# Opening a transformer block kernel: the channel attention of two batches interleaved, raw rows and centred weights

## The reference, cut to what matters

```python
x = x + attn_a(layernorm(x))     # channel attention, 8 heads of 16 channels
x = x + ffn(layernorm(x))        # 8 experts, 336 hidden units each, all computed
x = x + attn_b(layernorm(x))     # attention over the 512 rows
x = x + ffn(layernorm(x))

# attn_a: rms norm, then
qkv = einsum('bnc,oc->bno', xn, w_qkv)
q, k = l2norm(q), l2norm(k)      # over the 512 rows
sim = einsum('bhin,bhjn->bhij', q * exp(temperature), k)
out = einsum('bhij,bhjn->bhin', softmax(sim), v)
return einsum('bnc,oc->bno', out, w_out)
```

## Time and profile before

| | |
|---|---|
| median of 3 runs | 487.98 us (487.86 to 488.89) |
| the profiled execution | 489.73 us |
| its span in the trace | 487.9 us |
| PE busy | 476.1 us |
| PEld, DVE, ACT, POOL busy | 342.7, 303.0, 266.2, 312.4 us |
| first feed-forward product (`gu 0`) | 23.39 us after the span's start |

### The profile page before, as it was taken

How to read it: one execution, slowest core, us unless ns; L and a number is a source line. 1 busy time by engine, 2 the same in 40 slices (tenths; PEclk the granted TensorE clock), 3 DMA queues, 4 the chain that set the end, 5 groups by cost and what they waited for, 6 DMA issues and landing times.

```text
span 487.9 us, 6499 instructions
## 1 busy us (share of the span) xinstructions
PE 476.1 (98%) x2039; PEld 342.7 (70%) x2039; DVE 303.0 (62%) x718; ACT 266.2 (55%) x484; POOL 312.4 (64%) x326
## 2 busy tenths in 40 slices
PE   8899899999999999999999999999999999999997
PEld 7777666677676666666676766677676777778886
DVE  3656342646487768499836884359754565666563
ACT  3395636646724693348742649235772456456551
POOL 5355789336948576486463466467675586778774
PEclk9999899999999999999999999999999999999999
DMA  7700000000000000000000000000000000000000
GB/s 240 247 0 2 0 1 0 1 1 1 1 0 2 1 0 1 1 1 1 0 1 0 1 2 0 1 1 5 19 0 2 0 23 1 0 1 10 15 0 22
DMA packets 7933, 7.36 MB, mean 15 GB/s; under 512 B 732, under 2 KB 7772, under 8 KB 7900
## 3 DMA queue, kind: packets, MB, share of 16 engines
q1 hardware_dynamic: 7900, 6.96, 4.4%
HBM read 5.91 MB, written 1.05 MB: 14 GB/s over the span
## 4 chain that ended last, share of the span: by engine, by line
PE 83%; ACT 2%; DVE 1%; POOL 1%; issue 0%; ACTq 0%; DVEq 0%; POOLq 0%
PE bank L1313 21%; PE bank L1128 17%; PE bank L1130 17%; PE bank L1129 17%; PE bank L1351 3%; PE bank L1249 1%; PE bank L1343 1%; PE bank L1151 1%; PE bank L1363 1%; PE bank L1321 1%; PE bank L1257 1%; PE bank L1291 1%; ACT L778 1%; PE bank L1239 0%; PE bank L1219 0%
## 5 line engine op out<-in xcount | busy, mean ns | idle before, releaser
L647 POOL TENSOR_TENSOR t<-t,sl 128x512 f32<-128x512 f32 x105 | 148.6, 1421 | 80.9 <-DVE t L1069 61.7
L778 ACT ACTIVATE sl<-bank 128x512 f32<-128x512 f32 x168 | 99.2, 596 | 126.3 <-PE bank L1130 114.5
L1313 PE MATMUL bank<-t,WD 128*128 128x512 f32 x256 | 126.0, 592 | 0.0
L1069 DVE TENSOR_TENSOR t<-bank,sbc 128x512 f32<-128x512 f32 x105 | 72.3, 689 | 72.2 <-PE bank L1130 70.5
L1128 PE MATMUL bank<-xhF,WGh 128*128 128x512 f32 x167 | 89.8, 538 | 1.0 <-ACT sl L778 0.9
L647 POOL TENSOR_TENSOR t<-t,sbc 128x512 f32<-128x512 f32 x63 | 79.4, 1288 | 0.2
L1069 DVE TENSOR_TENSOR t<-bank,sl 128x512 f32<-128x512 f32 x63 | 42.9, 686 | 55.8 <-ACT sl L778 30.0
L1128 PE MATMUL bank<-xhF,WUh 128*128 128x512 f32 x168 | 66.8, 397 | 1.1 <-DVE t L1069 1.1
L1130 PE MATMUL bank<-xhF,WUl 128*128 128x512 f32 x168 | 66.3, 395 | 0.0
L1129 PE MATMUL bank<-xlF,WUh 128*128 128x512 f32 x168 | 66.3, 394 | 0.0
L1130 PE MATMUL bank<-xhF,WGl 128*128 128x512 f32 x167 | 66.2, 397 | 0.0
(11 more groups left out here) (210 smaller groups left out, 722.9 us busy)
## 6 DMA issues: line engine op xcount, KB each, us to landing
stage<-in_gate SPq DMA_DIRECT2D x7, 192.0 KB, 5.7
stage<-in_up SPq DMA_DIRECT2D x7, 192.0 KB, 5.7
WD<-in_down SPq DMA_DIRECT2D x7, 192.0 KB, 5.7
X<-in_x SPq DMA_DIRECT2D x4, 256.0 KB, 5.4
out<-X SPq DMA_DIRECT2D x3, 256.0 KB, 2.3
raw<-in_small SPq DMA_DIRECT2D x1, 384.0 KB, 4.2
out<-X SPq DMA_DIRECT2D x2, 128.0 KB, 1.9
raw<-in_small SPq DMA_DIRECT2D x1, 192.0 KB, 2.7
```

The source lines that it names most:

```text
L647: pool.tensor_tensor(t2[k % NT2][:, :], t2[k % NT2][:, :], by[:, :], ALU.mult).then_inc(a_done, 1)
L778: act.activation(sl[k % NSL][:, :], bank[k % 2][:, :], ACT.Silu).then_inc(silu_done, 1)
L1069: dve.tensor_tensor(t2[k % NT2][:, :], bank[2 + k % 2][:, :], by[:, :], ALU.mult).then_inc(t2_done, 1)
L1313: r = pe.matmul(OACC[:, :], WD[:, c, :], t2[k % NT2][:, :], start=(c == 0), stop=(c == CH - 1 or k == TAIL[0] - 1))
```

## The change

Batch 0 and batch 1 both run through the whole channel attention in the hand-written opening, interleaved. `A1_STEPS` is gone.

- The rows are not normalised for the attention. The weights for q, k and v are multiplied on PE by a centred matrix (`cenw`: 1/128 minus the identity, times the norm weight): step `wn`, one product of 128 x 384 and a ScalarE copy. The Gram matrix is of raw rows with rows scaled by 1/(variance term) (`rinv`, two small VectorE operations in place of GpSimd's power); the transposes are of raw `X`; the factor `rstd` is applied when the result is added to x.
- Batch 0 has no `am2`: its values are projected first (step `vT`, one 128 x 512 product, into the tile `YT`), and `y` uses `mix` directly.
- The sums of squares are a step of their own (`asq`), in other banks.
- The head mask is written in three operations on 128 columns.
- Warming is 4, 3, 2 and 8 products at four places.
- A step `silu` applies Silu to one column, into a tile that nobody reads, ahead of the first real one.
- The transfer of the small columns and that of batch 1's rows are issued earlier.

```diff
-WARM = (12, 2, 4, 7, 10)
+PRELUDE = [("warm", 0), ("xT", "A", 0), ("stats", "A", 0), ("rstd", "A", 0), ("wn", 0), ("xn", "A", 0), ("ag", 0),
...
+WARM = (4, 3, 2, 8)
-A1_STEPS = [(2, "asim"), (3, "ass"), (3, "apow"), (4, "ascale"), (7, "asT"), (7, "amax"), (8, "aexp"), (9, "awo"),
-            (11, "am"), (12, "am2"), (14, "y")]
...
             sp.dma_start(X[:, 0:NT, :], xv[:, 0]).then_inc(x_loaded[0], 16)
+            sp.dma_start(cols[:, :], cols_d).then_inc(cols_loaded, 16)
             sp.dma_start(raw[:, 0:C_OUT], small_d[:, 0:C_OUT]).then_inc(qkv_loaded, 16)
-            sp.dma_start(cols[:, :], cols_d).then_inc(qkv_loaded, 16)
+            sp.dma_start(X[:, NT:2 * NT, :], xv[:, 1]).then_inc(x_loaded[1], 16)
...
+            own = hmask[:, :].rearrange("p (e d) -> p e d", d=DH)
+            chain(pool.memset(hmask[:, :], 0.0))
+            chain(pool.affine_select(out=own, in_=own, compare_op=ALU.is_ge, fill=NEG, base=0,
+                                     pattern=[[-DH, H], [0, DH]], channel_multiplier=1))
+            pool.affine_select(out=own, in_=own, compare_op=ALU.is_ge, fill=NEG, base=DH - 1,
+                               pattern=[[DH, H], [0, DH]], channel_multiplier=-1).then_inc(consts_ready, 1)
...
+            act.activation(cenw[:, :], cenw[:, :], ACT.Identity, scale=cols[:, 0:1]).then_inc(cenw_ready, 1)
...
+                if kind == "wn":
+                    act.wait_ge(wn_full, 1)
+                    act.activation(raw[:, 0:C_OUT], bank[2][:, 0:C_OUT], ACT.Copy).then_inc(wn_ready, 1)
+                if kind == "vT":
+                    act.wait_ge(vT_full, 1)
+                    act.activation(YT[:, :], bank[0][:, :], ACT.Copy).then_inc(vT_ready, 1)
+                if kind == "silu":
+                    act.activation(junk[:, :], cols[:, 5:6], ACT.Silu)
...
+            dve.tensor_scalar(cenw[:, :], ident[:, :], 1.0 / D, None, ALU.subtract).then_inc(ci_ready, 1)
...
+                    if seq < 2:
+                        rinv = rinvs[seq]
+                        dve.wait_ge(stats_ready, seq + 1)
+                        chain(dve.tensor_scalar(rinv[:, :], mv[:, :, 1], 1.0 + RMS_EPS, RMS_EPS * LN_EPS, ALU.mult, ALU.add))
+                        chain(dve.reciprocal(rinv[:, :], rinv[:, :]))
...
+                    if seq < 2:
+                        for i in range(NT):
+                            dve.tensor_scalar(xn[:, i, :], X[:, NT * q + i, :], rinvs[seq][:, i:i + 1], None, ALU.mult).then_inc(xn_ready, 1)
+                        continue
...
+                    if s == ("y", 1):
+                        dve.wait_ge(rstd_ready, 2)
+                        for i in range(NT):
+                            x_ = X[:, NT + i, :]
+                            r = dve.scalar_tensor_tensor(x_, m_bank(t)[:, i * P:i * P + P], rstds[1][:, i:i + 1], x_, ALU.mult, ALU.add)
...
+                if kind == "wn":
+                    pe.wait_ge(cenw_ready, 1)
+                    pe.wait_ge(qkv_loaded, 16)
+                    pe.matmul(bank[2][:, 0:C_OUT], cenw[:, :], raw[:, 0:C_OUT], start=True, stop=True).then_inc(wn_full, 1)
+                if kind == "vT":
+                    pe.wait_ge(wn_ready, 1)
+                    wait_free(pe, turn_of["xT", "A", 0])
+                    pe.matmul(bank[0][:, :], raw[:, C_QKV + 256:C_QKV + 384], xaT[0][:, :], start=True, stop=True).then_inc(vT_full, 1)
```

More of the change, by code:

```diff
@@ L150, in needs @@
     if kind == "xT" and s[1] == "A":
-        return [("y", b - 2), ("ag", b)]
-    if kind == "am2" and b == 0:
+        return [("y", b - 2), ("ag", b)] if b > 1 else []
+    if kind == "am2" and b == 1:
         return [("wv", 0)]
@@ L165, in needs @@
         return [("byx", prev)] + [("bexp", b, i) for i in range(NT)]
-    return {"ag": [("ar", prev)], "ar": [("asim", prev)], "ass": [("ascale", prev)],
+    return {"ag": [("ar", prev)], "ar": [("asim", prev)], "ass": [("ascale", prev)], "asq": [("ar", b)],
             "ascale": [("asT", prev), ("amax", prev)], "amax": [("aexp", prev)], "aexp": [("am", prev)], "awo": [("am", prev)],
-            "am": [("am2", prev)], "am2": [("y", prev)],
+            "am": [("am2" if prev else "y", prev)], "am2": [("y", prev)],
             "bqk": [("bs", prev, NT - 1)], "bs": [("bpT", prev, NT - 1)],
@@ L378, in build @@
         ones = sb("ones", [P, 1])
+        junk = sb("junk", [P, 1])
+        cenw = sb("cenw", [P, P])
+        rinvs = [sb(f"rinv{i}", [P, NT]) for i in range(2)]
         hmask = sb("hmask", [P, P])
@@ L731, in _ @@
                     if b:
-                        wait_full(act, turn_of["am2", b - 1])
+                        wait_full(act, turn_of["am2" if b > 1 else "y", b - 1])
                     wait_full(act, t)
@@ L1177, in _ @@
                       .then_inc(m_full[t % 3], 1)
+                if kind == "asq":
+                    b = s[1]
+                    wait_free(pe, turn_of["ar", b])
+                    for j in range(2):
+                        r = pe.matmul(bank[1 + 2 * b][:, P + j:P + j + 1], qsq[:, 1 - j, :], ones[:, :], start=True, stop=True)
+                    r.then_inc(squares_full, 1)
                 if kind == "asim":
@@ L1182, in _ @@
                     wait_free(pe, turn_of["ar", b])
[L1183 to L1190 removed]
+                    r = pe.matmul(m[:, 0:P], raw[:, C_QKV + P:C_QKV + 2 * P], gw[:, 0, :], start=True, stop=True)
+                    if b > 1:
+                        for j in range(2):
+                            r = pe.matmul(m[:, P + j:P + j + 1], qsq[:, 1 - j, :], ones[:, :], start=True, stop=True)
                     r.then_inc(m_full[t % 3], 1)
@@ L1218, in _ @@
                         to = m[:, a] if b else bank[i][:, 0:P]
-                        r = pe.matmul(to, xaT[b % 2][:, a], mixw[:, :], start=True, stop=True)
+                        r = pe.matmul(to, xaT[b % 2][:, a] if b else YT[:, a], mixw[:, :] if b else mix[:, :], start=True, stop=True)
                         if b == 0 and i < NT - 1:
```

109 lines of the change are left out of this document (51 added, 58 removed).

## The result

The changed kernel takes 504.7 us (median of 4 runs, 504.08 to 506.31) against 488.08 for the kernel before on the same chip: ratio 1.0335, 95% interval 1.0315 to 1.0355. It is 3.35% slower, where 486.1 was forecast and 489.8 was the end of the range. The profiled execution has a span of 502.8 us, 14.9 more than the 487.9 before. The medians lie 16.6 apart: the profiled execution of the kernel before, with 489.73 us, was 1.7 above its median, and that of the changed kernel, with 504.96, only 0.3.

What follows compares the result with a forecast made beforehand. PE, busy 476.1 of 487.9 us, was taken as the bound. The terms +1.0 + 2.1 - 1.4 - 3.5 - 0.4 (xn wait) + 0.3 = -1.9 took the median 487.98 to 486.1 us, range 483.6 to 489.8.

Steps and rivals of the forecast that it cites:

- Slots 12 to 14 ... So -3.5 of the 3.8: Slots 12 to 14: of 3.8 us lost there, 3.5 are won as batch 1's attention work leaves; one bank late by 0.3.
- Slots 15 to 101 are planned in another order; before, this stretch lost next to nothing. +0.3.: Slots 15 to 101: the new order of steps costs only 0.3 us, priced from the calm before.
- The start of the chain, the interleaving, the end of the opening (+1.0): Opening: earlier xn and one round fewer before y, but ScalarE's queue decides; slot 0 starts at 24.4, 1.0 us late.
- The queue's sum: End of the opening: ScalarE's copies, table load, Silu, batch 1's wo to mixw, weight pieces and xhF add up to 24.4.
- the choice of the row: Opening: table load priced at its profiled 1.28 us, without the skill page's 1.38 us drain, which would raise the forecast 1.4.
- Slots 0 to 8 (+2.1): Slots 0 to 8: PE waits 2.85 us for Silu ahead of slot 3, further waits follow; +2.1 us net.
- PE work that leaves the slots (-1.4): Slots: am and am2, 0.25 each, and y, 0.9, leave PE's work there; 1.4 us saved.
- masks (0): Opening: the head mask's 24 operations end while GpSimd waits or before anybody needs them; nothing gained or lost.
- A: Slot 12: ScalarE jams, PE idles some 2 us, the clock falls, the 3.8 us stay; 489.9 us, chance 0.2.
- B: Opening and behind it: ScalarE keeps up, table load runs in a gap, slot 0 at 23.1; 483.8 us, chance 0.18.
- C: Opening: too little warming keeps PE at the low clock, costing 2.0 us; 488.1 us, at most 489.1, chance 0.17.
- D: Opening: interleaving yields nothing before slot 0, batch 1's work only moves there from a full PE; forecast contains it, no chance given.

Runs made afterwards that it cites:

- Experiment 11: Changed kernel with the turns wqk, wvp and wa of the mixer's weights held to slots 14 to 16: 499.86 us, ratio 1.0221.
- experiment 1: Also written e1_late: changed kernel with only batch 1's feed-forward thread started at slot 14 instead of at once: 483.89 us, ratio 0.9902.
- Experiment 3: Changed kernel, thread still early, other steps from slot 21 held to their former slots (GpSimd products and down steps not held): 494.83 us, ratio 1.0123.
- experiment 7: Also written e7_bs_hold: e2_route_late with batch 0's first scores (bs) held until slot 43: 488.94 us, ratio 1.0000.
- e2_route_late: Changed kernel with batch 1's feed-forward normalisation left early, only its router and scores moved to slots 21 to 32: 492.7 us, ratio 1.0083.
- experiment 4: Kernel before with only the head mask changed, three operations on 128 columns instead of 24: 488.38 us, ratio 1.0004.
- experiment 5: Kernel of experiment 1 with the dummy Silu that loads ScalarE's table placed right behind batch 1's exp: 484.9 us, ratio 0.9904.
- e6_late_silu_wp: This is experiment 6: kernel of experiment 5 with two weight pieces also moved behind xhF of batch 0: 484.12 us, ratio 0.9886.
- e8_warm: This is experiment 8: kernel of experiment 1 with 16 instead of 8 warming passes at the start: 484.67 us, ratio 0.9897.
- experiment 10: Changed kernel with late thread, xn at slot 16, 16 warming passes, earlier Silu table, two weight pieces later, SWl before y's addition: 479.9 us, ratio 0.9815.

## Why the prediction was wrong, step by step

**The step that failed first: "Slots 12 to 14 ... So -3.5 of the 3.8".** Measured +4.0 there where -4.0 was forecast (with `am` and `am2`). The prediction looked at what had left this place and at ScalarE's queue, and found one bank "late by 0.3". It counted the exp pair of the router, but not that `rt` holds one of three banks until VectorE is through behind that very pair. Experiment 11 moves only the third turn and gets 4.9 us back; experiment 1 moves the router away, and slots 12 and 13 are free of waits and take 3.97 us. So the 3.8 us were there to be won; the step that failed is that nothing new would stand in their place.

**The second: "Slots 15 to 101 are planned in another order; before, this stretch lost next to nothing. +0.3."** Measured +6.4 from slot 14 to the end where -2.2 was forecast. That a calm stretch stays calm in another order was assumed, not worked out. Experiment 3 prices the displaced order at 8.9 us of span. Slots 42 to 48, with one collision of turns at slot 44, take 5.4 more than before; experiment 7 moves the collision away in e2_route_late and gets 3.6 to 3.8 back. The rest (1.2 for `xlF`, 1.9 for `bmp` later on, and what the clock does behind them) was not taken apart further.

**The start of the chain, the interleaving, the end of the opening (+1.0).** Measured +1.6. The queue's sum was the right mechanism: load at 19.92, `wo` at 21.32, pieces from 23.41, `xhF` at 24.23.

```profile
19.92 1.28 ACT L702 ACT_TABLE_LOAD   x1
21.21 0.20 ACT L702 ACTIVATE junk<-cols 128x1 f32<-128x1 f32 x1
21.32 0.39 ACT L735 ACTIVATE wo<-raw,ari 128x128 f32<-128x128 f32 x1
```

`y` started at 17.31 instead of 16.4, since `raw` held `wn` 1.03 us and `wn` and the Gram product ran at the low clock. Behind the load ScalarE goes on at once. The Trainium skill, page "ScalarE: Activation LUTs", section "What ACT_TABLE_LOAD costs", counts a drain of some 1.38 us on top; this trace does not have it, here or around the router's exp (52.88 to 55.71), so the choice of the row was right.

**Slots 0 to 8 (+2.1).** The wait was right in mechanism and size: PE waited 2.76 us for Silu ahead of slot 3 (forecast 2.85). That slot 9 then started 21.25 us behind slot 0 (forecast 21.2) is partly luck. From slot 3 on the prediction has 1.8 us of further waits and nothing for the clock; the trace has 0.16 us of idle time, and slot 3's six passes at the low clock take 2.70 us instead of 1.4. The two errors cancel. The 2.1 us were also read as the price of the change. They were the first sign of the thread that had moved; with the thread late slot 7 starts 12.87 us behind slot 0, as before (12.82; 16.62 in the changed kernel), and slot 9 16.70, 1.2 less than before.

**PE work that leaves the slots (-1.4) and masks (0).** No sign against either; the mask is measured alone in experiment 4, the work is not.

**The rivals.** A had the right place, a wait of PE at slot 12 and the clock falling there, and the right starter, the pair of loads. It named ScalarE's jam, priced the wait at about 2 us and did not carry it on to the bank. B did not come, and its start of slot 0 at 23.1 was too early for the load alone: experiment 5 takes the load out of the row and wins 1.07 us, which from 25.02 gives some 24.0 (an estimate); 22.26 is reached only with experiments 6 and 8 added, in experiment 10. e1_late lies near B's 483.8 for another reason, for its slot 0 starts at 25.21. C was right that warming was cut too far, and too dear: 1.1 us at slot 0, not 2.0. D holds for the opening by itself, as the prediction says there: work moves from the slots into it, and slot 0 comes later. Experiment 1 shows that this is worth 1% once the rest stays in place. The ends of the range, 483.6 and 489.8, are 0.2 and 0.1 off the rivals' own sums, 483.8 and 489.9.

## What to carry to other kernels

When a step that others depend on moves, list every step whose earliest slot it set, and look where each of them lands: here one `needs` entry had been the only thing that kept a thread in its good place, and its move cost 20 us, for an opening that is worth nearly 5. For buffers that go round in turns, write down for each long holder which step is third behind it; that position made the two longest unforeseen waits. And pin what worked (a start slot in the table) before an upstream part is made faster.

## What the hardware showed besides

A wait of the same length does not always cost the same: behind 1.75 us the granted clock stayed at 1.00 (2.4 GHz) in e1_late, behind 1.76 it fell to 0.70 over 3 us in e8_warm. The openings of e2_route_late and e7_bs_hold have the same steps in the same order, and yet the clock was 0.66 from 24 to 29 us in the first and 1.00 in the second, and slots 0 to 6 took 18.38 and 16.64 us. A page of the Trainium skill, "TensorE: Matmul & The Clock Gate", Part 1, says that how long a kernel stays at the low level varies from run to run. The kernel before agrees: beside experiments 1 to 4 its 13 runs have a mean granted clock of 1.000, 0.997 or 0.996, and spans from 486.0 us at 1.000 to 487.9 at 0.997. A gain under 2 us should therefore be read from the rows as well as from the time.

VectorE's `SWl` (128 x 128, both operands in SBUF) takes 1.05 us in e6_late_silu_wp, from 25.06 to 26.11, while GpSimd subtracts `WUl` from 24.96 to 25.96, and 0.28 us in the changed kernel, where it starts at 26.34 and GpSimd is done. Rows of GpSimd in e6_late_silu_wp and of VectorE in the changed kernel:

```profile
24.96 1.00 POOL L629 TENSOR_TENSOR WUl<-stage,WUh 128x384 fp32r<-128x384 f32 x1
```

```profile
26.34 0.28 DVE L927 TENSOR_TENSOR SWl<-raw,SWh 128x128 fp32r<-128x128 f32 x1
```

The VectorE operation before it, which reads a bank and `X` (0.34 us at 24.80), kept its pace beside GpSimd. That the two engines disturb each other on operands in SBUF was not tested by itself.
